# A graph-network block on one core: the batches of a software pipeline put in another order

## The chip, the cores and the metric

The kernel runs on one core of a Trainium2 chip. The metric is the device time of one execution in microseconds, the median of three runs. Every time below comes from those runs or from one profiled execution.

## What is computed

6250 nodes with 256 features each, and 106250 edges with 96 features, sorted by the node they point to (`dst`). For every node the edges that point to it are reduced in three ways, and a two-layer network is applied:

```
h    = maximum(layernorm(x), 0)                      # 6250 x 256
out1 = segment_sum(edge, dst); out2 = segment_max(edge, dst); out3 = out1 / count
cat  = concatenate([h, out1, out2, out3, u[0]], axis=1)
y    = relu(cat @ W1 + b1) @ W2 + b2                 # hidden size 1024
out  = x + (y + h)
```

## The kernel before

**Tiles.** 6250 nodes make 49 tiles: tile i holds one node for each of the 128 partitions, and within a partition the nodes are sorted by their number of edges, and each rank makes a tile. The tables `LOW` and `CAP` (49 entries each) say, for every tile, how many edge slots are always full and how many there can be. A tile with LOW = k1 and CAP = k1 + k2 has k1 + k2 slots of 96 numbers per partition; the k2 last ones are masked. Tiles 0 to 3 have 15 slots, 4 and 5 have 16, 26 and 27 have 21, 42 and 43 have 28, and the five heavy ones, 44 to 48, have 29, 31, 32, 35 and 40.

**Groups and batches.** `BATCHES` (line 44) is a list of 15 batches. A batch is one or two groups, and a group is a pair of tiles with equal LOW and CAP, or one heavy tile. A batch is so two, three or four tiles wide. Each group has its buffer: `ell[g % 2]` for its edges and `es[g % 2]` for its masked ones (both show as `work` in the trace).

**Stages.** The program is a software pipeline over the batches, written out by hand for each engine. In stage s, TensorE runs the two matrix layers of batch s in eight chunks of 128 hidden units (`layer1` of chunk C, L527, L531 and L536; then `layer2` of chunk C - 2, L547 and L551), and at the end of chunks 2, 3, 5 and 6 it transposes the first to fourth tile of batch s + 1 (`transposes`, L512 and L515). Between them the other engines run, in the same stage and cut into the same eight steps m = 0 to 7:

- VectorE: `lo` of the chunk before in every step (L821); then for batch s + 1 the tree of the first group (`tree_mid` in step 0, `tree_tail` in step 1, L736), `output` of batch s - 1 (L852) and `tree_head` of the second group (L725) in step 2, `tree_mid` and `tree_tail` of the second group in steps 3 and 4, `in_lo` of each tile in steps 3, 4, 6 and 7 (L825), `moments` of batch s + 2 in step 5, `residual` in step 6 (L838, L843), `scales` of batch s + 2 and `tree_head` of its first group in step 7.
- ScalarE: `relu` of the chunk in every step (L407 and L409); `norm` (L419), `means` (L426, L427) and `in_hi` (L434) of batch s + 1; and `mask` (L398), one instruction for each masked slot of a tile: that of the first group of batch s + 2 in steps 4 to 6, that of its second group half in step 7 and half in step 0 of the next stage.
- GpSimd: the gathers. `gather_x` (L301) of batch s + 2, one for each tile; `gather_group` (L308) of group g + 2 as soon as the tree of group g is done, four transfers for a pair and two for a single tile; `scatter` (L322) of batch s - 1, one for each tile.

Every engine works through its own list in order. What ties them: `layer1(C)` waits for `relu(C - 2)`, `layer2(C)` for `lo(C)`, `relu(C)` for `lo(C - 1)`, `transposes` of a tile for its `norm`, its `means` and the `in_lo` of the tile before, `means` for the tree of its group, and `mask` for the gather of its group. So TensorE can be some two chunks ahead of VectorE, and no more.

Of the kernel before, what the change touches and what calls it, by code (L numbers as in the profile page):

```python
# [16 lines left out]
def gnn_block(nc, x, dst, edge, u, W1, b1, W2, b2, out):  # L17
# [23 lines left out]
           22, 22, 23, 23, 24, 24, 24, 24, 25, 25, 27, 27, 28, 28, 29, 31, 32, 35, 40]  # L41
    assert len(LOW) == len(CAP) == PER

    BATCHES = [[(4, 5)], [(6, 7)], [(8, 9), (44,)], [(10, 11), (45,)], [(12, 13), (46,)], [(14, 15), (47,)], [(16, 17), (48,)],
               [(18, 19), (42, 43)], [(20, 21), (40, 41)], [(22, 23), (38, 39)], [(24, 25), (36, 37)], [(26, 27), (34, 35)],
               [(28, 29), (32, 33)], [(0, 1), (2, 3)], [(30, 31)]]
    NB = len(BATCHES)
    NCH = NB * HC
    groups, tiles = [], []
    g_of, t_of = [], []  # L50
    for b, gs in enumerate(BATCHES):
        g_of.append(list(range(len(groups), len(groups) + len(gs))))
# [9 lines left out]
    NG = len(groups)  # L62
    assert all(len(gs) <= 2 for gs in BATCHES)
    ELL, ES = 56, 26
# [862 lines left out]
```

How the kernel before makes its waits and increments, by code:

```python
        @block.sync  # L233
        def _(sp):
            sp.dma_start(sd[0:SR, 0:SC], dst_sd).then_inc(sd_in, 16)
            sp.wait_ge(seam_free, 2)
            sp.wait_ge(sd_in, 16)
            sp.dma_start(dstp[0:NS, :], dst.rearrange("(r c) -> r c", c=STEP)).then_inc(dstp_in, 16)
            sp.dma_start(dstp[NS:NS + WIN // STEP, :], tail[:, :]).then_inc(dstp_in, 16)
            sp.dma_start(sd[0:SR - 1, SC:SC + 1], dst_sd[1:SR, 0:1], allow_slow_non_contiguous=True).then_inc(seam_in, 16)
            sp.wait_ge(win_in, 16)
            for c in range(0, KC, 2):
                sp.dma_start(raw1[:, c * H:(c + 2) * H].rearrange("p (c h) -> p c h", h=H),
                             W1[c * P:(c + 2) * P, :].rearrange("(c p) h -> p c h", p=P)).then_inc(w1_in, 16)
# [3 lines left out]
            sp.dma_start(w1u, W1[K:K + G, :]).then_inc(c_in, 16)  # L248
            sp.dma_start(u0[:, :], u[0:1, :].rearrange("a g -> g a"), allow_slow_non_contiguous=True).then_inc(c_in, 16)
            sp.dma_start(b1c[:, :], b1.rearrange("(c p) -> p c", p=P), allow_slow_non_contiguous=True).then_inc(c_in, 16)
            sp.dma_start(b2b[:, :], b2.rearrange("(a d) -> a d", a=1).broadcast_to([P, D])).then_inc(c_in, 16)
            sp.wait_ge(flag_ready, 1)
            general = sp.value_load(flag[0:1, 0:1], min_val=0, max_val=1)
            with sp.If(general > 0):
# [11 lines left out]
        @block.gpsimd  # L267
# [21 lines left out]
            pool.memset(bad[:, :], 0.0).then_inc(consts, 1)  # L289
            pool.wait_ge(row_ready, 1)
            pool.wait_ge(dstp_in, 32)
```

## Time and profile before

| | us |
|---|---|
| median of 3 runs (lowest, highest) | 577.2 (576.81, 577.95) |
| the profiled execution, its own time | 576.6 |
| its span | 574.4 |
| TensorE busy in matmuls | 481.2 (84%) |
| VectorE busy | 470.0 (82%) |
| ScalarE busy | 351.0 (61%) |
| GpSimd busy | 242.0 (42%) |
| mean granted TensorE clock | 0.978 |

The shares are means over stages with different limits. The table of 40 slices shows TensorE at 9 tenths or more from slice 19 on, and between 4 and 9 tenths from slice 4 to 18. The start of layer 1 of each batch in the trace of TensorE gives the borders of the stages, and the stretch between two borders can be asked for the busy time of each engine.

### The profile page before, as it was taken

To read this page: it belongs to the slowest core of one execution; us is meant where nothing else is said; L and a number is where in the kernel's file an instruction comes from. 1 tells how busy PE (TensorE), PEld (TensorE's weight loads), DVE (VectorE), ACT (ScalarE), POOL (GpSimd) and SP (SyncE) were. 2 spreads that over 40 slices of the span, in tenths; PEclk is the share of its full clock that TensorE was granted. 3 is DMA by queue.
4 is the path that set the end of the run, shared out by engine and by line. 5 is a ranking of instruction groups with operands and counts; after the bars stand their busy time and mean duration, and the time that the engine had idled before them with its cause. 6 is when DMAs were issued, how large, how long until landed. Compare 5 with 4: busy or idle time off the path is not lost.

```text
span 574.4 us, 8775 instructions
## 1 busy us (share of the span) xinstructions
PE 481.2 (84%) x3016; PEld 443.3 (77%) x3016; DVE 470.0 (82%) x888; ACT 351.0 (61%) x951; POOL 242.0 (42%) x251
## 2 busy tenths in 40 slices
PE   0020569889999999877999999999999999999991
PEld 0020559889999899867988888888888888888991
DVE  4896768898998999989999998999989889793220
ACT  0934638676768586684856757667577685743330
POOL 2055430716182746645277274571752714202021
PEclk9999979898999999998999999999999999999997
DMA  2935430525253454733446245441550524001010
GB/s 79 287 97 172 139 132 2 171 100 181 100 165 142 152 182 141 246 105 126 157 147 212 70 137 193 151 167 66 184 199 15 158 90 156 34 0 38 1 38 18
DMA packets 18836, 71.12 MB, mean 124 GB/s; under 512 B 4571, under 2 KB 5755, under 8 KB 18776
## 3 DMA queue, kind: packets, MB, share of 16 engines
q0 software_dynamic: 15408, 65.72, 34.1%
q1 hardware_dynamic: 3378, 4.79, 2.8%
q8 instruction: 24, 0.39, 0.3%
q14 instruction: 26, 0.21, 0.1%
HBM read 64.09 MB, written 6.85 MB: 124 GB/s over the span
## 4 chain that ended last, share of the span: by engine, by line
PE 60%; DVE 15%; DMA 8%; ACT 7%; issue 5%; POOL 3%; SPq 0%; DVEq 0%; POOLq 0%; ACTq 0%
PE l1ps L527 24%; PE l1ps L531 12%; PE yps L547 11%; DVE work L736 9%; DMA work<-in_edge_attr,idx 6%; PE yps L551 6%; PE tps L512 3%; PE l1ps L536 3%; ACT work L398 3%; POOL work L308 2%; ACT cat L373 2%; DVE cat L736 1%; POOL out_y L322 1%; DMA work<-in_dst 1%; DVE inl L825 1%
## 5 line engine op out<-in xcount | busy, mean ns | idle before, releaser
L308 POOL DMA_INDIRECT work<-in_edge_attr,idx x98 | 118.4, 1208 | 202.5 <-DVE cat L736 153.3
L527 PE MATMUL l1ps<-inh,w1h 128*128 128x512 f32 (+2 forms) x480 | 173.8, 368 | 2.1 <-ACT hh L409 1.4
L527 PE MATMUL l1ps<-inh,w1l 128*128 128x512 f32 (+2 forms) x480 | 169.3, 359 | 0.0
L736 DVE TENSOR_TENSOR work<-work 128x768 f32<-128x768 f32 (+14 forms) x174 | 151.4, 902 | 1.1
L407 ACT ACTIVATE hf<-l1ps,b1e 128x512 f32<-128x512 f32 (+2 forms) x120 | 72.6, 605 | 108.2 <-PE l1ps L536 108.0
L398 ACT ACTIVATE work<-work,mk 128x96 f32<-128x96 f32 x435 | 122.5, 367 | 26.3 <-DMA work<-in_edge_attr,idx 26.0
L531 PE MATMUL l1ps<-inl,w1h 128*128 128x512 f32 (+2 forms) x480 | 112.9, 358 | 0.0
L821 DVE TENSOR_TENSOR hl<-hf,hh 128x512 fp32r<-128x512 f32 (+2 forms) x120 | 71.3, 594 | 42.8 <-ACT hh L409 37.1
L527 PEld LDWEIGHTS l1ps<-inh,w1h 128*128 128x128 f32 x480 | 92.7, 193 | 10.5 <-issue 2.0
L322 POOL DMA_INDIRECT out_y<-xr,oidx x49 | 68.3, 1393 | 77.1 <-DVE xr L852 63.0
L527 PEld LDWEIGHTS l1ps<-inh,w1l 128*128 128x128 f32 x480 | 93.0, 194 | 7.8
L547 PE MATMUL yps<-w2h,hh 128*128 128x256 f32 x392 | 98.5, 282 | 0.0
L547 PE MATMUL yps<-w2l,hh 128*128 128x256 f32 x392 | 98.1, 281 | 0.0
L531 PEld LDWEIGHTS l1ps<-inl,w1h 128*128 128x128 f32 x480 | 85.6, 193 | 10.3
L547 PEld LDWEIGHTS yps<-w2h,hh 128*128 128x128 f32 x392 | 74.3, 190 | 2.6
L547 PEld LDWEIGHTS yps<-w2l,hh 128*128 128x128 f32 x392 | 74.4, 190 | 2.4
L409 ACT ACTIVATE hh<-l1ps,b1e 128x512 fp32r<-128x512 f32 (+2 forms) x120 | 72.0, 600 | 0.0
L725 DVE TENSOR_TENSOR work<-work 128x1344 f32<-128x1344 f32 (+15 forms) x52 | 71.1, 1367 | 0.9
L551 PE MATMUL yps<-w2h,hl 128*128 128x256 f32 x392 | 66.2, 282 | 2.5 <-DVE hl L821 2.5
L301 POOL DMA_INDIRECT xr<-in_x,nid x49 | 51.3, 1047 | 36.1 <-DVE nid L643 21.5
L512 PE MATMUL tps<-ident,cat 128*128 128x128 f32 x196 | 31.3, 284 | 41.5 <-ACT cat L427 38.4
L512 PEld LDWEIGHTS tps<-ident,cat 128*128 128x128 f32 x196 | 22.7, 145 | 44.9 <-DVEq L786 34.5
(126 smaller groups left out, 478.5 us busy)
## 6 DMA issues: line engine op xcount, KB each, us to landing
work<-in_L_gnn_W SPq DMA_DIRECT2D x3, 1024.0 KB, 7.4
work<-in_edge_attr,idx POOLq DMA_INDIRECT x98, 5.3
xr<-in_x,nid POOLq DMA_INDIRECT x49, 4.0
out_y<-xr,oidx POOLq DMA_INDIRECT x49, 3.1
work<-in_dst SPq DMA_DIRECT2D x1, 415.0 KB
dstp<-in_dst SPq DMA_DIRECT2D x1, 415.0 KB
work<-in_L_gnn_W SPq DMA_DIRECT2D x3, 128.0 KB, 7.5
xr<-in_L_gnn_W SPq DMA_DIRECT2D x1, 256.0 KB, 11.1
```

The costliest lines, as they stand in the source:

```text
L308: pool.indirect_dma_start(out=ell[g % 2][:, at:at + kk * F], out_offset=None, in_=edge, in_offset=bass.IndirectOffsetOnAxis(ap=idx[:, a + ...
L322: pool.indirect_dma_start(out=out, out_offset=bass.IndirectOffsetOnAxis(ap=oidx[:, i:i + 1], axis=0), in_=xr[:, b % XS, k, :], in_offset=None,
L398: last = act.activation(es[g % 2][:, at * F:(at + 1) * F], ell[g % 2][:, src:src + F], ACT.Copy, scale=mk[:, a + j, e:e + 1])
L407: act.activation(hf[C % 2][:, 0:cols], l1ps[C % 2][:, 0:cols], ACT.Relu, bias=b1e[:, m:m + 1])
L409: act.activation(hh[C % 3][:, 0:cols], l1ps[C % 2][:, 0:cols], ACT.Relu, bias=b1e[:, m:m + 1]).then_inc(hi_done, 1)
L512: pe.transpose(tps[:, ks(c)], cat[:, k, ks(c)], ident[:, :])
L527: pe.matmul(ps, wt[:, c, ks(m)], inh[b % 2][:, c, 0:cols], start=(c == 0 and wt is w1h), stop=False)
L531: pe.matmul(ps, w1h[:, c, ks(m)], inl[b % 2][:, c, 0:cols], start=False, stop=False)
L547: pe.matmul(ybank(b, j)[:, j % 2 * D:(j % 2 + 1) * D], hh[C % 3][:, ks(j)], wt[:, m, :], start=(m == 0 and j % 2 == 0 and wt is w2h), stop ...
L551: last = pe.matmul(ybank(b, j)[:, j % 2 * D:(j % 2 + 1) * D], hl[C % 3][:, ks(j)], w2h[:, m, :], start=False, stop=(m == HC - 1), skip_gro ...
L736: return V.tensor_tensor(out=slots(buf, n, per, 0, size // 2) if out_ is None else out_, in0=slots(buf, n, per, 0, size // 2), in1=slots(b ...
L821: V.tensor_tensor(out=hl[C % 3][:, 0:cols], in0=hf[C % 2][:, 0:cols], in1=hh[C % 3][:, 0:cols], op=ALU.subtract).then_inc(lo_done, 1)
```

## The change

Only the list of batches is another. The widths before are 2, 2, 3, 3, 3, 3, 3, 4, 4, 4, 4, 4, 4, 4, 2; now they are 2, 2, 2, 4, 4, 3, 3, 4, 3, 4, 3, 4, 4, 4, 3: the same count of each width. The pairs that stand together and the partner of each heavy tile change too; groups, tables and all functions stay as they are.

```diff
-    BATCHES = [[(4, 5)], [(6, 7)], [(8, 9), (44,)], [(10, 11), (45,)], [(12, 13), (46,)], [(14, 15), (47,)], [(16, 17), (48,)],
-               [(18, 19), (42, 43)], [(20, 21), (40, 41)], [(22, 23), (38, 39)], [(24, 25), (36, 37)], [(26, 27), (34, 35)],
-               [(28, 29), (32, 33)], [(0, 1), (2, 3)], [(30, 31)]]
+    BATCHES = [[(4, 5)], [(6, 7)], [(8, 9)], [(10, 11), (12, 13)], [(14, 15), (16, 17)], [(18, 19), (45,)], [(20, 21), (46,)],
+               [(28, 29), (42, 43)], [(22, 23), (47,)], [(30, 31), (40, 41)], [(24, 25), (48,)], [(32, 33), (38, 39)],
+               [(0, 1), (2, 3)], [(34, 35), (36, 37)], [(26, 27), (44,)]]
```

Two places show what it moves, both on VectorE. The first is steps 2 to 4 of the last stage in which TensorE runs a batch of two. Before, that is stage 1, and the batch that is made ready has three tiles, the third of them tile 44 (`hl` is `lo`, `work` the tree, `inl` is `in_lo`):

```order
L821 TENSOR_TENSOR hl<-hf,hh 128x256
L852 TENSOR_TENSOR xr<-yps,xr 128x512
L725 TENSOR_TENSOR work<-work 128x1056
L725 TENSOR_TENSOR work<-work 128x672
L821 TENSOR_TENSOR hl<-hf,hh 128x256
L825 TENSOR_TENSOR inl<-tps,inh 128x4x128
L736 TENSOR_TENSOR work<-work 128x1344
L736 TENSOR_TENSOR work<-work 128x480
```

Now it is stage 2, and the batch that is made ready has four tiles, with (12, 13) as its second group:

```order
L821 TENSOR_TENSOR hl<-hf,hh 128x256
L852 TENSOR_TENSOR xr<-yps,xr 128x512
L725 TENSOR_TENSOR work<-work 128x1536
L725 TENSOR_TENSOR work<-work 128x2x192
L821 TENSOR_TENSOR hl<-hf,hh 128x256
L825 TENSOR_TENSOR inl<-tps,inh 128x4x128
L736 TENSOR_TENSOR work<-work 128x2x864
L736 TENSOR_TENSOR work<-work 128x2x384
```

The single tile's tree gave way to a pair's, which goes on for one more tile in every step behind it, while `lo` stays 256 columns wide.

The second is steps 2 to 4 of stage 8. Before, TensorE runs a batch of four there, and (38, 39) is the second group of the next batch:

```order
L821 TENSOR_TENSOR hl<-hf,hh 128x512
L852 TENSOR_TENSOR xr<-yps,xr 128x512 x2
L725 TENSOR_TENSOR work<-work 128x1728
L725 TENSOR_TENSOR work<-work 128x2x672
L821 TENSOR_TENSOR hl<-hf,hh 128x512
L825 TENSOR_TENSOR inl<-tps,inh 128x4x128
L736 TENSOR_TENSOR work<-work 128x2x1152
L736 TENSOR_TENSOR work<-work 128x2x384
```

Now TensorE runs a batch of three, and the second group is (40, 41):

```order
L821 TENSOR_TENSOR hl<-hf,hh 128x384
L852 TENSOR_TENSOR xr<-yps,xr 128x512 x2
L725 TENSOR_TENSOR work<-work 128x1920
L725 TENSOR_TENSOR work<-work 128x2x672
L821 TENSOR_TENSOR hl<-hf,hh 128x384
L825 TENSOR_TENSOR inl<-tps,inh 128x4x128
L736 TENSOR_TENSOR work<-work 128x2x1248
L736 TENSOR_TENSOR work<-work 128x2x480
```

`lo` became 384 columns wide and the tree of the second group a little larger; the stage that has to cover it is TensorE's for three tiles, not for four. Stages 6 and 10 are now of the same kind.

## Rows read from the trace of the kernel before

**Rows 1.** Windows: stages 0 to 8 and 14, borders at layer 1 of each batch.

```profile
core 0: us, PE busy (x) PEld busy (x) DVE busy (x) ACT busy (x) POOL busy (x), PEclk, DMA share, GB/s
65.20:92.80 27.60, 21.39 (x151) 20.73 (x152) 20.89 (x51) 17.86 (x58) 9.17 (x10) 0.88 0.37 124
92.80:117.60 24.80, 21.45 (x169) 21.10 (x169) 22.69 (x43) 17.86 (x56) 12.70 (x11) 0.93 0.42 133
117.60:149.10 31.50, 29.42 (x187) 29.25 (x186) 28.52 (x61) 21.32 (x61) 12.49 (x11) 0.95 0.43 147
149.10:178.20 29.10, 28.63 (x193) 28.46 (x192) 26.92 (x51) 21.32 (x61) 14.74 (x12) 1.00 0.44 145
178.20:208.50 30.30, 28.98 (x194) 28.46 (x193) 28.60 (x55) 21.72 (x62) 16.52 (x13) 1.00 0.44 146
208.50:239.80 31.30, 28.93 (x193) 28.42 (x193) 30.02 (x56) 22.38 (x65) 16.42 (x13) 1.00 0.44 146
239.80:278.10 38.30, 31.32 (x199) 30.61 (x198) 33.81 (x53) 24.33 (x71) 20.34 (x17) 0.96 0.50 173
278.10:316.10 38.00, 37.45 (x217) 32.36 (x216) 36.04 (x61) 25.86 (x69) 20.96 (x16) 1.00 0.44 150
316.10:353.90 37.80, 37.80 (x223) 33.05 (x221) 34.61 (x56) 25.53 (x68) 20.26 (x16) 1.00 0.44 151
...
541.90:563.00 21.10, 20.85 (x178) 20.65 (x176) 5.59 (x12) 6.73 (x17) 3.89 (x4) 1.00 0.07 26
```

**Rows 2.** TensorE's timeline in stage 0: first matmuls of two chunks, two tiles.

```profile
88.26 0.28 PE L527 MATMUL l1ps<-inh,w1h 128*128 128x256 f32 x1
...
90.49 0.28 PE L527 MATMUL l1ps<-inh,w1h 128*128 128x256 f32 x1
```

**Rows 3.** Chain that ended last: start, us; chunks of three tiles, then four.

```profile
171.68 1.39 PE l1ps L527 x8
...
175.01 1.41 PE l1ps L527 x8
...
344.61 1.87 PE l1ps L527 x8
...
347.64 0.95 PE yps L547 x8
348.59 0.47 PE yps L551 x4
...
349.61 1.87 PE l1ps L527 x8
...
354.06 1.87 PE l1ps L527 x8
```

**Rows 4.** Groups of instructions by form, VectorE: two sizes of the tree.

```profile
L725 DVE TENSOR_TENSOR work<-work 128x1344 f32<-128x1344 f32 x18 | 28.0, 1555 | 0.2
L736 DVE TENSOR_TENSOR work<-work 128x384 f32<-128x384 f32 x41 | 22.5, 550 | 0.1
```

**Rows 5.** VectorE's timeline in stage 6: first `lo`, then two tree pieces of (42, 43).

```profile
242.86 0.56 DVE L821 TENSOR_TENSOR hl<-hf,hh 128x384 fp32r<-128x384 f32 x1
...
253.25 3.74 DVE L725 TENSOR_TENSOR work<-work 128x2112 f32<-128x2112 f32 x2
...
258.10 4.08 DVE L736 TENSOR_TENSOR work<-work 128x2688 f32<-128x2688 f32 x2
```

**Rows 6.** TensorE's timeline: waits before transposes, one in stage 1, two in stage 6.

```profile
101.76 0.63 PE L512 MATMUL tps<-ident,cat 128*128 128x128 f32 x4 [2.18 <-ACT cat L427]
...
252.94 0.63 PE L512 MATMUL tps<-ident,cat 128*128 128x128 f32 x4 [1.93 <-ACT cat L427]
...
268.72 0.63 PE L512 MATMUL tps<-ident,cat 128*128 128x128 f32 x4 [2.97 <-ACT cat L427]
```

**Rows 7.** GpSimd's timeline: first gather of group (42, 43).

```profile
231.90 1.28 POOL L308 DMA_INDIRECT work<-in_edge_attr,idx  x1 [1.31 <-DVE cat L736]
```

**Rows 8.** ScalarE's timeline: first half of that group's mask.

```profile
243.36 3.04 ACT L398 ACTIVATE work<-work,mk 128x96 f32<-128x96 f32 x11 [3.37 <-DMA work<-in_edge_attr,idx]
```

**Rows 9.** GpSimd's timeline: the last scatter of the run.

```profile
565.55 0.97 POOL L322 DMA_INDIRECT out_y<-xr,oidx  x1 [0.30 <-issue]
```

## The prediction

> **What bounds the kernel now.** I read first the busy time by stage [rows 1], since the shares of the whole run mix stages with different limits. Behind the window and its length stand the busy times of PE, PEld, DVE, ACT and POOL, then TensorE's granted clock. What has to be seen is how much of a stage is more than TensorE needs at its full clock. That need comes from the starts of successive chunks: a chunk of a batch of two takes 90.49 - 88.26 = 2.23 us [rows 2], of three 175.01 - 171.68 = 3.33, of four 354.06 - 349.61 = 4.45, and 349.61 - 344.61 = 5.00 where a tile is transposed behind it, so 0.55 for a tile [rows 3]. Layer 2 is 0.95 + 0.47 = 1.42 us of a chunk of four, 0.355 for a tile, and the first two chunks of a stage carry layer 2 of the batch before. So a stage needs 8 chunks + 0.55 x (tiles of the next batch) + 0.71 x (width before - own width). For stage 8 this gives 35.6 + 2.2 = 37.8, which is its length to the tenth [rows 1]. The other stages, length less need:
>
> - stage 0: 27.6 - 17.6 = 10.0 (nothing precedes it: 1.4 less); stage 1: 24.8 - 19.6 = 5.2; stage 2: 31.5 - 27.6 = 3.9; stage 3: 29.1 - 28.4 = 0.7; stage 4: 30.3 - 28.4 = 1.9; stage 5: 31.3 - 28.4 = 2.9; stage 6: 38.3 - 28.9 = 9.4; stage 7: 38.0 - 37.1 = 0.9; stages 8 to 13: nothing; stage 14: 21.1 - 20.7 = 0.4.
>
> Together 35.3 us are lost, all but 1.3 in stages 0 to 6. The rest is TensorE's work, and that is the same in both orders: the same count of each width. So the change can give at most 35 us, and it is worth what it does to these losses.
>
> Next, who takes them. In stage 6 VectorE is busy 33.8 us against TensorE's need of 28.9: it runs three tiles and makes four ready. TensorE waits there before transposes, 1.93 and 2.97 us among others [rows 6], for `means`, which wait for the tree; two steps of the tree take 3.74 and 4.08 us [rows 5]. In stage 8 VectorE is busy 34.6, but TensorE needs 37.8 and covers it. Stages 1 to 5 are nearly even (VectorE 22.7 to 30.0), with losses to match. The rule to take along: a stage loses where the batch that runs is narrower than the batch that is made ready. Before this happens twice (2 to 3 tiles in stage 1, 3 to 4 in stage 6). The new order does it four times: 2 to 4 in stage 2, 3 to 4 in stages 6, 8 and 10.
>
> Two more things add to stage 6. VectorE enters it late: the stage begins at 239.8, its first `lo` at 242.86 [rows 5], 3 us behind. And the gather of (42, 43), issued from 231.90 [rows 7], is there only at 243.36, where the mask has made ScalarE wait 3.37 us [rows 8]; `relu` is queued behind that mask, and `lo` and TensorE's next chunks behind `relu`. Last, the clock: the stages with long waits show a granted clock of 0.88 to 0.96, the others 1.00 [rows 1]; in stage 6, 4% of 38.3 is 1.5 us, part of its 9.4.
>
> **The change stage by stage** (new losses).
>
> - Up to the end of stage 0: the first two batches and their gathers are the same, **10.0** stays. `moments` in it has one tile less, hidden behind the same waits.
> - Stage 1 (2 tiles, makes 2 ready): the work for tile 44 is gone. The 2.18 us wait of the first transposes [rows 6] is for (8, 9), and that stays. Bounds: 2.2, only this wait, and 5.2, no gain. I take **4.0**, nearer the upper end, as the halved clock comes with the wait.
> - Stage 2 (2 tiles, makes 4 ready) has no counterpart; the nearest is the old stage 1, VectorE busy 22.7 in 24.8. A size of the tree costs 0.15 us + 1.05 ns for an element: (1555 - 550) / 960 from two forms [rows 4]. By this the tree of (12, 13) is 8.3 us against 7.2 for tile 44: + 1.1; one more `in_lo` + 0.6, `residual` + 0.5, `moments` + 0.45, the rest + 0.35. So 25.7 busy and the same 2.1 idle: 27.8 against a need of 17.8 + 2.2 = 20.1, 7.7 lost. The edges of (14, 15), asked for in step 4 some 9 us after their gather is issued, can come late by 1 to 2 us, since such a gather takes 11.5 [rows 7, 8]; in return VectorE may end late into the wide stage 3. I take **8.0**; bounds 5.0 (three more us spill into stage 3) and 11.0 (nothing spills, late edges in full and more clock).
> - Stages 3 to 5 (4 to 4, 4 to 3, 3 to 3): TensorE covers VectorE as in stage 8, save the last, like the old stage 3. **1.4** in place of 0.7 + 1.9 + 2.9; bounds 0.3 and 4.0.
> - Stage 6 (3 to 4) is the old stage 6 with (28, 29) for (18, 19): by the size rule 0.6 us more tree. But VectorE enters it some 2 us late, not 3, as stage 5 follows on a wide stage, and the mask waits less by some 2 us, half of it felt. **8.5**; bounds 6.0 and 10.0.
> - Stage 8 (3 to 4) need: 26.7 + 2.2 + 0.7 = 29.6. Here VectorE enters in step, at most 0.7 us late, since stage 7 is wide. I walk it from the start of the stage. Steps 0 to 4 hold five `lo` (2.5), the middle and tail of (30, 31) (6.7), `output` (1.2), all of the tree of (40, 41) (12.1), two `in_lo` (1.2): 23.7, done at 24.4, with `means` some 25. TensorE comes to the transposes of that group's first tile after six chunks, two transposes and the extra layer 2: 20.0 + 1.1 + 0.7 = 21.8. It waits 3 us. The last tile costs a few tenths, the halved clock behind the wait up to 1.5. **4.5**; bounds 1.5 and 9.4 (as the old stage 6).
> - Stage 10 (3 to 4): the tree of (38, 39) is 0.8 us less, but the mask of (0, 1), 26 slots in place of 14, stands in steps 4 to 6 on ScalarE, ahead of `in_hi` of the third tile. **5.0**; same bounds.
> - Stages 7, 9 and 11 to 14: at most the 0.9 of the old stage 7 each. **1.4** in all; bounds 0.5 and 3.0.
>
> New losses: 10.0 + 4.0 + 8.0 + 1.4 + 8.5 + 4.5 + 5.0 + 1.4 = 42.8, against 35.3: **+ 7.5**.
>
> - The end: three scatters in place of two behind the last `output`; one is 0.97 + 0.30 = 1.27 us [rows 9]. **+ 1.3**. The order of the other gathers moves no queue onto the path: GpSimd is busy at most 55% of a stage [rows 1], and its waits are for the tree.
>
> 576.6 + 7.5 + 1.3 = **585.4** for an execution like the profiled one. That one stands 0.6 us under the median of the runs, 577.2, less than they scatter; I keep 585.4.
>
> One rule weighed: the gather of (42, 43) moves 56 slots of 48 KB, 2.75 MB, and took 11.5 us from the first issue to the mask [rows 7, 8]. The Trainium skill (DMA: Bandwidth & Descriptors, Anatomy of one DMA — SWDGE (gpsimd) path) gives some 2.0 us fixed and the bytes at 436 GB/s, which makes an estimate of 8.3 us. By that no mask in stage 6 would wait and the sum would be some 1.5 us less, 583.9; the row decides.
>
> **Rivals.**
>
> 1. *The lag is absorbed, and the run gets faster.* TensorE may be two chunks ahead of VectorE, 6.7 us in a batch of three, and after each narrow stage a wide one follows in which VectorE catches up at some 3 us a stage (37.8 against 34.6). If waits begin only when those two chunks are used up, and not at the transposes, stages 8 and 10 lose 1.5 each, stage 6 6.0, stage 2 5.0, stage 1 2.2, the others 0.8: 27.0. The time is 576.6 - 8.3 + 1.3 = 569.6. For it: stages 1 to 5, where VectorE was 90% or more busy, lost little. Against: all three waits of [rows 6] are at transposes, which depend on VectorE directly. It decides if the third tile's `means` are done less than 22 us into stage 8. Chance 0.14.
> 2. *Each step from three to four costs what the old one did.* If lag, late mask and clock come back each time, stages 6, 8 and 10 lose 9.4 each, stage 2 11.0: 10.0 + 5.2 + 11.0 + 1.4 + 28.2 + 1.4 = 57.2, so 576.6 + 21.9 + 1.3 = 599.8. For it: the only sample. Against: that sample began 3 us late and with a late gather, which a wide stage before it should spare. Chance 0.18.
> 3. *The losses only change places*: early stages (2 to 5 lost 9.4) give what 8 and 10 take, and the time is 577 to 578. Chance 0.05.
>
> **Numbers.** The forecast gets 0.63. The likeliest case gives 585.4. The range goes from 573, which leaves out most of the first rival, to 600, which takes in the second to its price: 573 to 600. A measurement of this kernel tells about 0.2% (1.2 us). Faster by more: the first rival and a little of the forecast's lower side, 0.16; within: 0.04; slower: 0.80.
>
> **What would show it.** In the profile after: stages 6, 8 and 10 are 37.4, 34.1 and 34.6 us long, each with a wait of TensorE of 2 us or more before the transposes of the third tile; stage 2 is some 28 us with VectorE busy nearly throughout; stages 3, 4, 7, 9 and 11 to 13 have no waits worth naming; layer 1 of batch 0 begins at 65.2 as before. If stages 8 and 10 come out under 31 us the walk is wrong, and the slack between the engines is larger than I took it; if they are 38 or more, lag does not die out in a wide stage.

## The result and the profile after

The changed kernel takes 586.2 us (median of 4 runs, 585.36 to 586.5) against 577.58 for the kernel before in the same comparison: a ratio of 1.0147, interval 1.0132 to 1.0163. It is slower by 8.6 us. The prediction said 585.4, and 8.8 us more for an execution like the profiled one.

The same windows as in [rows 1], of the changed kernel, all 15 stages (columns as there):

```profile
65.50:94.40 28.90, 23.53 (x151) 23.14 (x152) 20.43 (x49) 17.96 (x58) 11.06 (x12) 0.88 0.40 129
94.40:115.70 21.30, 19.12 (x164) 18.95 (x164) 17.32 (x40) 13.78 (x41) 8.51 (x9) 1.00 0.34 107
115.70:143.90 28.20, 23.26 (x174) 22.89 (x173) 25.48 (x46) 20.81 (x65) 17.01 (x15) 0.88 0.51 162
143.90:181.20 37.30, 36.56 (x211) 31.67 (x210) 33.20 (x60) 25.14 (x66) 12.63 (x12) 1.00 0.35 115
181.20:218.50 37.30, 37.30 (x218) 32.55 (x217) 31.33 (x54) 22.57 (x59) 14.84 (x14) 1.00 0.36 124
218.50:247.60 29.10, 29.10 (x199) 29.10 (x199) 26.96 (x54) 20.95 (x58) 16.58 (x15) 1.00 0.51 171
247.60:284.60 37.00, 30.98 (x197) 30.47 (x197) 34.17 (x50) 24.38 (x71) 17.49 (x14) 0.95 0.44 150
284.60:321.10 36.50, 36.50 (x211) 31.75 (x210) 33.66 (x63) 23.63 (x62) 17.69 (x14) 1.00 0.44 155
321.10:356.10 35.00, 31.70 (x205) 31.36 (x205) 32.38 (x51) 24.02 (x69) 18.30 (x14) 0.95 0.43 146
356.10:392.60 36.50, 36.50 (x211) 31.77 (x211) 34.52 (x60) 25.02 (x68) 19.95 (x15) 1.00 0.46 152
392.60:426.30 33.70, 30.15 (x204) 29.64 (x203) 30.88 (x48) 25.99 (x78) 18.90 (x16) 1.00 0.38 116
426.30:465.00 38.70, 37.52 (x217) 32.45 (x216) 34.86 (x64) 27.42 (x75) 17.04 (x15) 1.00 0.45 151
465.00:503.10 38.10, 37.87 (x221) 32.97 (x221) 35.71 (x54) 24.70 (x65) 13.95 (x10) 1.00 0.31 106
503.10:540.40 37.30, 37.30 (x218) 32.55 (x217) 26.77 (x39) 18.36 (x41) 5.82 (x4) 1.00 0.04 14
540.40:570.20 29.80, 29.80 (x202) 29.61 (x200) 6.45 (x11) 8.45 (x17) 3.90 (x4) 1.00 0.05 19
```

Where TensorE's busy time (first after the comma) is the stage's length, nothing or nearly nothing is lost: stages 4, 5, 7, 9, 13, 14. Apart from the start (stages 0 and 1), the stages in which a narrow batch runs while a wider one is made ready (2, 6, 8, 10) are those with a large gap. With the need of each stage from the prediction's rule:

| stage | widths | lost, forecast | lost, measured |
|---|---|---|---|
| 0 | 2 to 2 | 10.0 | 28.9 - 17.5 = 11.4 |
| 1 | 2 to 2 | 4.0 | 21.3 - 18.9 = 2.4 |
| 2 | 2 to 4 | 8.0 | 28.2 - 20.0 = 8.2 |
| 3 to 5 | 4, 4, 3 to 3 | 1.4 | 1.0 |
| 6 | 3 to 4 | 8.5 | 37.0 - 28.8 = 8.2 |
| 8 | 3 to 4 | 4.5 | 35.0 - 29.6 = 5.4 |
| 10 | 3 to 4 | 5.0 | 33.7 - 29.6 = 4.1 |
| 7, 9, 11 to 14 | | 1.4 | 2.3, of it 1.6 in stage 11 |
| all | | 42.8 | 43.0 |

These are all waits of TensorE in stages 6, 8 and 10, from its timeline (the bracket is the idle time before the row, and what ended it); they answer to [rows 6]:

```profile
259.40 0.63 PE L512 MATMUL tps<-ident,cat 128*128 128x128 f32 x4 [1.61 <-ACT cat L427]
264.87 0.63 PE L512 MATMUL tps<-ident,cat 128*128 128x128 f32 x4 [1.42 <-DVE inl L825]
275.28 0.63 PE L512 MATMUL tps<-ident,cat 128*128 128x128 f32 x4 [2.99 <-ACT cat L427]
...
336.69 0.63 PE L512 MATMUL tps<-ident,cat 128*128 128x128 f32 x4 [0.73 <-DVE inl L825]
346.68 0.63 PE L512 MATMUL tps<-ident,cat 128*128 128x128 f32 x4 [2.57 <-ACT cat L427]
...
408.13 0.63 PE L512 MATMUL tps<-ident,cat 128*128 128x128 f32 x4 [0.75 <-DVE inl L825]
417.51 0.63 PE L512 MATMUL tps<-ident,cat 128*128 128x128 f32 x4 [1.93 <-ACT cat L427]
422.44 0.63 PE L512 MATMUL tps<-ident,cat 128*128 128x128 f32 x4 [0.86 <-DVE inl L825]
```

All are before transposes, and the longest of each stage is that of the third tile (275.28, 346.68, 417.51), as the walk through stage 8 had it.

VectorE enters stage 8 only 322.18 - 321.1 = 1.1 us behind, with the `lo` of the last chunk of four tiles, and stage 10 0.8 us behind (393.41 - 392.6). It enters stage 6 3.2 us behind (250.76 - 247.6), like the old stage 6 [rows 5]:

```profile
250.76 0.56 DVE L821 TENSOR_TENSOR hl<-hf,hh 128x384 fp32r<-128x384 f32 x1
...
322.18 0.69 DVE L821 TENSOR_TENSOR hl<-hf,hh 128x512 fp32r<-128x512 f32 x1
```

At the end stand three scatters, the last issued at 574.30 against 565.55 before [rows 9]; from the end of TensorE's work to the end of the last scatter's issue it is 575.3 - 570.2 = 5.1 us against 566.5 - 562.8 = 3.7.

### The profile page after: what moved, and what is told of

The parts are those of the page before. It is cut to its first block, busy times and chain, and to the rows that moved or that the text cites. A ratio compares the mean times of both kernels' runs of the same rounds, so it can differ in the third digit from the quotient of the medians.

```text
span 583.2 us, 8775 instructions
## 1 busy us (share of the span) xinstructions
PE 484.2 (83%) x3016; PEld 446.8 (77%) x3016; DVE 471.3 (81%) x888; ACT 351.1 (60%) x951; POOL 238.2 (41%) x251
## 4 chain that ended last, share of the span: by engine, by line
PE 61%; DVE 17%; ACT 8%; DMA 5%; issue 4%; POOL 2%; SPq 0%; DVEq 0%; POOLq 0%; ACTq 0%
PE l1ps L527 24%; PE l1ps L531 12%; PE yps L547 12%; DVE work L736 9%; PE yps L551 6%; PE tps L512 4%; DMA work<-in_edge_attr,idx 3%; ACT work L398 3%; PE l1ps L536 3%; ACT cat L373 2%; DVE work L725 2%; POOL work L308 2%; DVE inl L825 1%; DVE cat L736 1%; DMA work<-in_dst 1%
## 5 line engine op out<-in xcount | busy, mean ns | idle before, releaser
L308 POOL DMA_INDIRECT work<-in_edge_attr,idx x98 | 115.8, 1181 | 210.3 <-DVE cat L736 178.7
L736 DVE TENSOR_TENSOR work<-work 128x576 f32<-128x576 f32 (+11 forms) x174 | 151.7, 903 | 1.1
L322 POOL DMA_INDIRECT out_y<-xr,oidx x49 | 66.0, 1347 | 79.6 <-DVE xr L852 65.6
L512 PE MATMUL tps<-ident,cat 128*128 128x128 f32 x196 | 32.5, 292 | 47.6 <-ACT cat L427 41.6
```

The source lines that it names most:

```text
L308: pool.indirect_dma_start(out=ell[g % 2][:, at:at + kk * F], out_offset=None, in_=edge, in_offset=bass.IndirectOffsetOnAxis(ap=idx[:, a + ...
L512: pe.transpose(tps[:, ks(c)], cat[:, k, ks(c)], ident[:, :])
L736: return V.tensor_tensor(out=slots(buf, n, per, 0, size // 2) if out_ is None else out_, in0=slots(buf, n, per, 0, size // 2), in1=slots(b ...
```

## The experiments

The first four ran together on one chip (12), with the kernel before beside them at 578.46 us. The changed kernel was not among them, so the ratio to the kernel before is what is compared: 1.0147 for the changed kernel. A difference of 1 to 2 us found in this way is small: the kernel before itself stood 0.9 us higher here than in the first comparison. So the traces are set beside it; that of the changed kernel has a span of 583.2 us and loses 43.0.

A single stage is less steady than the whole. These are two stages 1 that run the same program, of the run with fewer masks below and of the changed kernel on a later chip; in the changed kernel's first trace the stage takes 21.30 us at a granted clock of 1.00:

```profile
93.80:116.70 22.90, 20.72 (x164) 20.55 (x163) 17.32 (x40) 13.81 (x41) 9.56 (x10) 0.93 0.34 105
...
95.80:121.00 25.20, 21.91 (x165) 21.72 (x164) 17.66 (x41) 14.12 (x43) 9.80 (x10) 0.86 0.33 103
```

So the same stage loses 2.4, 4.0 or 6.2 us, TensorE's busy time rises with the loss, and its granted clock falls. Stage 6 loses 8.2 in the changed kernel's first trace and 6.9 in the run with fewer masks, which leaves it alone.

**VectorE's work taken out of the narrow stages** (part of the computation is left out)

```diff
+    LIGHT = (3, 7, 9, 11)
 ...
                 dve.wait_ge(masked, g + 1)
+                if g in [g_of[b][1] for b in LIGHT]:
+                    V.tensor_tensor(out=s[:, 0:1], in0=s[:, 0:1], in1=e[:, 0:1], op=ALU.add).then_inc(dve_step, 1)
+                    dve.wait_ge(dve_step, next(step))
+                    return
```

> The changed kernel without the first piece of the tree (L725) of the second group of batches 3, 7, 9 and 11, the four whose preparation stands in a stage narrower than they are; one column is added in its place, so that the output of these tiles is not the reference's. This takes 2.3 + 3.7 + 3.6 + 3.4 = 13.0 us from VectorE. Theory A (VectorE's work in the narrow stage is what TensorE waits for): stages 2, 6, 8 and 10 lose 8.1, 8.2, 5.3 and 4.2 us now and fall by 2 to 3.5 each, 10 to 12 us in all, so about 575. Theory B (late gathers and masks on ScalarE hold these stages): under 3 us less, 583 or more.

Measured: 574.67 us, ratio 0.9938 (0.9921 to 0.9955). Against 1.0147 that is 2.1% or 12.1 us less, for 12.6 us less of VectorE's busy time (458.7 against 471.3). Windows of stages 2, 6, 8 and 10:

```profile
115.60:142.40 26.80, 22.25 (x175) 21.73 (x174) 23.42 (x45) 21.32 (x68) 14.85 (x14) 0.94 0.52 166
246.10:279.10 33.00, 30.88 (x198) 30.53 (x198) 30.09 (x47) 24.25 (x71) 16.49 (x14) 0.95 0.46 161
315.60:346.40 30.80, 29.88 (x205) 29.71 (x204) 28.02 (x46) 24.15 (x69) 17.14 (x14) 1.00 0.45 160
383.10:415.00 31.90, 30.00 (x205) 29.66 (x204) 27.85 (x47) 25.95 (x78) 18.55 (x16) 1.00 0.40 123
```

They are 1.4, 4.0, 4.2 and 1.8 us shorter than in the changed kernel. VectorE's busy time in them is less by 2.1 to 4.4 us, GpSimd's by 0.4 to 2.2, and ScalarE's is the same within 0.5. The sum came out as expected; of the single stages two gave more than the 2 to 3.5 expected, and two less.

The edit also lets the gathers behind these trees start sooner, so the waits of ScalarE for edges have to be looked at. In stage 2 that wait fell by 1.1 us, from 2.59 to 1.49, and the stage gained 1.4: there the two causes can't be told apart. In stages 6, 8 and 10 the waits grew, from 2.08 to 2.48, from none to 0.44 and from 0.59 to 1.37, while the stages became shorter:

```profile
133.77 1.44 ACT L399 ACTIVATE work<-work,mk 128x96 f32<-128x96 f32 x5 [1.49 <-DMA work<-in_edge_attr,idx]
...
248.81 3.04 ACT L399 ACTIVATE work<-work,mk 128x96 f32<-128x96 f32 x11 [2.48 <-DMA work<-in_edge_attr,idx]
...
403.28 2.24 ACT L399 ACTIVATE work<-work,mk 128x96 f32<-128x96 f32 x8 [1.37 <-DMA work<-in_edge_attr,idx]
```

So Theory B falls for stages 6, 8 and 10.

**The same work taken out of wide stages** (the same edit for batches 4, 8, 10 and 13; part of the computation is left out)

> The same piece left out for the second group of batches 4, 8, 10 and 13, whose preparation stands in a stage that is at least as wide (stages 3, 7, 9 and 12), some 10.5 us of VectorE's work; the output of these tiles is not the reference's. Theory A: those stages are TensorE's and lose 0.9, 0, 0 and 0.4 us, so at most 1.3 us less, 585 to 586. Rival C (VectorE's total counts, wherever it stands): 8 to 10 us less, 577.

Measured: 585.11 us, ratio 1.0121 (1.0104 to 1.0138), 1.5 us less than the changed kernel by the ratios, with intervals that overlap. Stages 3, 7 and 9 keep their length to the tenth, stage 12 loses nothing in place of 0.4, and the span of the trace is 583.2 as in the changed kernel. VectorE's total is nearly the same before and after the change (470.0 and 471.3 us); 9.3 us taken from it are worth at most 1.5 in one place, 12.6 are worth 12 in the other. Rival C falls.

**Fewer masks on ScalarE** (part of the computation is left out)

```diff
+                first, end = n * k2 * piece // pieces, n * k2 * (piece + 1) // pieces
+                if g in [g_of[b][1] for b in (9, 11)]:
+                    end = first + 1
-                for at in range(n * k2 * piece // pieces, n * k2 * (piece + 1) // pieces):
+                for at in range(first, end):
```

> The changed kernel with 2 masks each in place of 20 and 18 for the second groups of batches 9 and 11, so 34 instructions and some 9.5 us less on ScalarE, at the borders of stages 7/8 and 9/10; the output of these tiles is not the reference's. Theory A: 0 to 1.5 us less, since relu follows a mask only in step 0. Theory B: stages 8 and 10 lose their 9.5 us of waits, 577 to 580.

Measured: 586.09 us, ratio 1.0137 (1.0118 to 1.0157): no difference that can be told, for 9.2 us less of ScalarE's busy time (341.9 against 351.1). Stage 8 loses 5.4 as before, and stage 10 4.7 where it lost 4.1. The masks in steps 4 to 6 were left as they are, so this says nothing of them.

**One step up in place of three**

```diff
-               [(28, 29), (42, 43)], [(22, 23), (47,)], [(30, 31), (40, 41)], [(24, 25), (48,)], [(32, 33), (38, 39)],
+               [(22, 23), (47,)], [(24, 25), (48,)], [(28, 29), (42, 43)], [(30, 31), (40, 41)], [(32, 33), (38, 39)],
```

> The changed order with batches 8 and 10 moved to stand behind batch 6, so that the widths are 2,2,2,4,4,3,3,3,3,4,4,4,4,4,3 and there is one step from three to four in place of three. Theory A: the losses of stages 8 and 10 (5.3 + 4.2) go, two stages from three to three cost 2 to 3 each, and the one step that is left costs 8.5 to 9.5, as VectorE enters it late: about 4 us less, 582. Rival 1 of the prediction (lag is absorbed anyway): no change, 586. If steps were all that counted and stages from three to three cost nothing: 577.

Measured: 584.93 us, ratio 1.0114 (1.0096 to 1.0132), 1.9 us less by the ratios; expected were 4. In the traces the losses are 42.4 in place of 43.0, so most of the 1.9 may be noise. Its stages 6 to 9, with widths 3 to 3, 3 to 3, 3 to 4, 4 to 4:

```profile
249.40:279.80 30.40, 28.94 (x193) 28.42 (x192) 28.47 (x52) 21.63 (x62) 15.51 (x13) 1.00 0.43 151
279.80:312.30 32.50, 29.03 (x193) 28.52 (x192) 30.80 (x57) 22.46 (x65) 16.39 (x14) 1.00 0.45 153
312.30:349.40 37.10, 31.13 (x198) 30.59 (x197) 34.48 (x52) 24.30 (x71) 18.82 (x16) 0.95 0.47 164
349.40:388.90 39.50, 37.58 (x216) 32.35 (x216) 37.40 (x64) 26.42 (x71) 21.75 (x17) 1.00 0.48 165
```

The one step costs 37.1 - 28.8 = 8.3, close to the 8.5 that the prediction had for a step that VectorE enters late. But the two stages from three to three cost 2.1 and 4.2, since they make the batches with tiles 47 and 48 ready, and the wide stage behind the step still loses 2.4, which I had left out: VectorE is busy 37.4 us in it and pays off what it owes. Narrow stages in a row build up a debt; alternating ones pay it each time. So the number of steps up is not what counts by itself: these four stages lose 17.0 us with one step, and stages 6 to 10 of the changed kernel 17.7 with three.

**The step up early, and the narrow batches behind the wide ones.** Two orders that follow from theory A. The first begins with two batches of two, so that its step up stands in stage 1; the second begins with one, so that it stands in stage 0. This is the second:

```diff
+    BATCHES = [[(4, 5)], [(8, 9), (10, 11)], [(22, 23), (42, 43)], [(24, 25), (40, 41)], [(26, 27), (38, 39)], [(28, 29), (36, 37)],
+               [(30, 31), (34, 35)], [(0, 1), (2, 3)], [(12, 13), (48,)], [(14, 15), (47,)], [(16, 17), (46,)], [(18, 19), (45,)], [(20, 21), (44,)],
+               [(32, 33)], [(6, 7)]]
```

> A new order with the same groups' sizes: widths 2,2,4,4,4,4,4,4,4,3,3,3,3,3,2, so one step up (2 to 4, in stage 1, with the light pairs (8, 9) and (10, 11)) and from there on no stage narrower than the batch it makes ready. Theory A: stage 0 loses 10 to 11, stage 1 8 to 9.5, the stages of four together 3, the four from three to three 1 to 2 each, the end as before: 28 in all against 35 before, so 5 to 9 us faster than the kernel before, ratio 0.984 to 0.991. Rival C (the total of VectorE's work counts, whatever the order): as before, 1.00.

Measured: 575.76 us (8 runs), ratio 0.9953 (0.9936 to 0.997): faster than the kernel before by 2.7 us, where 5 to 9 were expected. Its trace is of its slowest run (578.11). Stage 1 loses 8.2, as expected, but stage 0 12.5, stage 2 4.5, and stages 10 to 13 3.0, 1.4, 2.5 and 3.9.

> The same with the step up already in stage 0: widths 2,4,4,4,4,4,4,4,3,3,3,3,3,2,2. Theory A: stage 0 takes on the work for two more tiles (some 11 us of VectorE's) on top of its 10 us, of which part are waits in which the work does not fit: it loses 17 to 21; stage 1 nothing, the two stages of two at the end 0 to 2. In all 27 to 32: 0.984 to 0.995 of the kernel before.

Measured: 570.55 us, ratio 0.9868 (0.9854 to 0.9883): inside the expectation, and 7.7 us faster than the kernel before. The parts were partly luck. Stage 0 with four tiles to make ready loses 12.6, not 17 to 21; but stage 1, which was to lose nothing, loses 4.5, like the stage behind the step in the order before. The two together make 17.1: part of the debt is paid one stage on.

Both orders also change which groups stand together and put the heavy tiles into the narrow batches, and both end with two scatters in place of three, like the kernel before. What they share cancels between the two of them: the step in stage 0 in place of stage 1 is worth 5.2 us.

**Two repairs of the changed order that gave nothing**

```diff
+                    late = 1 if s == 2 else 0
-                    if 4 <= m < 7 and ahead:
-                        mask(ahead[0], m - 4, 3)
+                    if 4 + late <= m < 7 + late and ahead:
+                        mask(ahead[0], m - 4 - late, 3)
```

> The changed kernel with the three pieces of the mask of (14, 15) in stage 2 in steps 5, 6 and 7 in place of 4, 5 and 6, so that ScalarE does not wait for their edges (2.59 us) ahead of means. VectorE ends the tree of (12, 13) at 135.1, the transposes start at 137.0: stage 2 gets 1.1 us shorter, the rest the same: 0.5 to 1.5 us less than the changed kernel. If the late edges were the whole wait: 2.7 us less.

> The changed order with batches 12 and 13 in exchange, so that the 26 masks of (0, 1) stand in stage 11 (four tiles) and no more in stage 10 (three tiles). The prediction put 0.5 to 1.2 us of stage 10 down to them. Theory A: stage 10 loses 3.2 to 4.0 in place of 4.2, and the 1.5 of stage 11 goes: 1 to 2 us less in all. If masks do not count: no change.

Measured: 593.42 us for both, ratios 1.0258 (1.0242 to 1.0274) and 1.0265 (1.0249 to 1.028), 7 us above the changed kernel where 0.5 to 2 below were expected. They and the two orders before ran together on another chip (13). The exchanged order is slower already in stages 0 to 2, where its program is that of the changed kernel. So I ran four kernels side by side once more.

> The order with batches 12 and 13 in exchange once more. In its first run it took 593.4 us, and its trace shows what no trace before it shows: TensorE's signal that a chunk is ready reached ScalarE 2 to 5 us after the last matmul of the chunk at a dozen places, stage 0 among them, in which its program is that of the changed kernel. Theory D (those late signals come with the chip or the load, not with the order): 584 to 585.5 us now, no such late signal, stage 10 at 3.2 to 4.0 us of loss. Rival E (they belong to this kernel's program): 593 again.

> The changed kernel once more, beside the others. Theory D: like its first runs, 586, unless this chip shows the late signals, and then in all four kernels of this call. Rival E: 586 while the exchanged order stays at 593.

> The kernel before as a kernel of its own, for its trace on this chip: 577 to 579 us; its trace shows late signals only if Theory D's chip is the one that is drawn.

> The order with the step up in stage 0 once more. It took 570.6 us with a dozen late signals. Theory D: without them the stages of four tiles lose nothing, and the run is 3 to 7 us shorter, 563 to 567. Rival E: 570.5 again.

Measured, on chip 10: the exchanged order 592.56 us (1.0248), the changed kernel itself 592.74 (1.0235, 1.0214 to 1.0256), the kernel before 578.39 (0.9998), the step up in stage 0 570.40 (0.9859). So rival E falls: the changed kernel is at 593 here too. Theory D's first half fits: the late signals are in all four kernels that ran here, and in none of chip 12. Its numbers fell, since this chip showed them too. But each chip was used for one set of runs, so the chip and anything else that went with the set can't be told apart. `relu` in stage 0 on ScalarE's timeline, the changed kernel in its first trace:

```profile
83.47 0.47 ACT L407 ACTIVATE hf<-l1ps,b1e 128x256 f32<-128x256 f32 x1 [2.18 <-PE l1ps L536]
87.13 0.47 ACT L407 ACTIVATE hf<-l1ps,b1e 128x256 f32<-128x256 f32 x1 [0.68 <-PE l1ps L536]
89.36 0.48 ACT L407 ACTIVATE hf<-l1ps,b1e 128x256 f32<-128x256 f32 x1 [0.33 <-PE l1ps L536]
```

and on chip 10:

```profile
83.75 0.47 ACT L407 ACTIVATE hf<-l1ps,b1e 128x256 f32<-128x256 f32 x1 [2.18 <-PE l1ps L536]
90.33 0.47 ACT L407 ACTIVATE hf<-l1ps,b1e 128x256 f32<-128x256 f32 x1 [3.48 <-PE l1ps L536]
92.13 0.46 ACT L407 ACTIVATE hf<-l1ps,b1e 128x256 f32<-128x256 f32 x1
```

TensorE's timeline has the last matmul of that chunk at 86.81 in the first and at 86.68 on chip 10; there `relu` starts 3.4 us after it ends. Of what `relu` waits for, the `lo` of VectorE had ended at 85.0, so it isn't that:

```profile
86.68 0.28 PE L536 MATMUL l1ps<-inr,w1r 96*128 96x256 f32 x1
```

Differences of a few us can be read only between kernels that ran together. Beside the changed kernel on chip 10 the exchanged order gains 0.2 us, within the noise. Its stage 10 loses 4.9 in place of 5.8, and its stage 11 2.0 in place of 1.6. Beside the later mask on chip 13, which leaves these stages as they were, stage 10 loses 5.6 in place of 5.7. So what the 26 masks of (0, 1) cost in stage 10 lies between nothing and some 1 us, and isn't settled; the prediction's sum has 1.3 for them (5.0 - 4.5 + 0.8).

The later mask shortens the wait that it was made for: in stage 2 the third tile waits 1.70 us, against 2.48 in the exchanged order beside it. In stage 3 the first tile now waits 2.55 us, against 0.73 in the changed kernel's first trace, and the stage loses 4.9 in place of 0.9. VectorE's `tree_head` had waited 2.12 us for the mask there. How much of that is the edit's isn't shown, since a late signal stands in front of the same mask (`relu` at 149.83, after 1.83 us).

## Why the prediction was right

- **The rule.** A stage loses where the batch that runs is narrower than the one made ready: all four places came out, within 1 us each, and no other stage but 0, 1 and 11 lost more than 1. The pair of runs without `tree_head` shows that it is VectorE's work in stages 6, 8 and 10; in stage 2 the late edges may have a part. That each stage hit within 1 us is in part luck, since a stage of the same program moved by 1.3 to 3.8 us between traces.
- **The walk through stage 8.** It had the tree of (40, 41) done at 24.4 us into the stage and the wait for the third tile at 3 us; in the trace the last piece of that tree ends at 345.8 - 321.1 = 24.7, and the wait is 2.57, as TensorE comes 1.2 us later than in the walk. VectorE was 1.1 us behind at the start where 0.7 was taken. The lag does die out in a wide stage, which fits stage 8's 5.4 against the old 9.4. Rival 1 falls (the third tile's `means` came after 22 us), rival 2 falls, and so does rival 3, which had the time at 577 to 578. One sign just missed: stage 10's wait is 1.93, not 2 or more.
- **Stage 6.** 37.0 us, forecast 37.4, but not by the forecast's way. VectorE was to enter it 2 us late and entered it 3.2 us late, and the mask's wait was to be some 2 us shorter and was 1.3 us shorter. Both would have made it more than 8.5; it lost 8.2. The gather of (42, 43) took its 11.4 us again (issued at 238.45, its mask at 249.81 after a wait of 2.08 us). So the row was the right price. By the formula of the Trainium skill (DMA: Bandwidth & Descriptors, Anatomy of one DMA — SWDGE (gpsimd) path) the estimate had been 8.3 us, and this trace doesn't agree with it. The four issues alone, which follow one another on GpSimd, take 5.1 us here (238.45 to 243.51).
- **Stage 2.** 28.2 us, forecast 28.1. The late edges of (14, 15) made ScalarE wait 2.59 us there, more than the 1 to 2 I had.
- **Stages 0 and 1** missed by 1.4 and 1.6, in opposite directions. In stage 1 the halved clock that I had charged did not come in this trace: its granted clock is 1.00. In two runs of chip 12 (fewer masks, and one step up in place of three), with the same program there, it is 0.93 and the stage loses 4.0, as forecast. In stage 0 the halved clock came while TensorE worked and not while it waited. Two windows, 75 to 80 and 80 to 85, of the kernel before:

```profile
75.00:80.00 5.00, 1.69 (x7) 1.42 (x8) 3.49 (x8) 1.76 (x6) 1.22 (x2) 0.51 0.00 0
80.00:85.00 5.00, 5.00 (x37) 5.00 (x36) 1.92 (x4) 2.38 (x6) 3.51 (x4) 0.81 0.91 311
```

and of the changed one:

```profile
75.00:80.00 5.00, 1.15 (x5) 0.97 (x6) 3.71 (x9) 1.51 (x6) 0.97 (x2) 0.84 0.00 0
80.00:85.00 5.00, 5.00 (x26) 4.99 (x25) 1.54 (x3) 1.76 (x4) 3.78 (x5) 0.50 0.85 258
```

- **Stage 11** lost 1.6 where nearly nothing was forecast, as the lag of stage 10 spills over; the "rest" of 1.4 was too small by 0.9. **The end**: + 1.3 forecast, + 1.4 measured. **The start**: layer 1 of batch 0 begins at 65.5, not at 65.2.

So the sum hit within 1 us partly because errors of up to 1.6 cancelled. And it holds for the first comparison: on chip 10 the change costs 2.35% (592.74 us), which the range still takes in.

## What to carry to other kernels

In a pipeline that works on batch s and makes batch s + 1 ready, look at the width of the batch that is made ready against the width of the one that runs. Where the first is the larger, the engine that prepares has more work than the stage covers (here such stages lose 4 to 8 us each), and its slack in a wide stage before can't be saved up. Merging the steps up into one is not enough: one step behind two narrow stages cost nearly as much as three steps. What helped was to put the step into the start, where the bound engine waits anyway; that order is 1.3% faster than the kernel before, and on chip 10, beside it, 3.8% faster than the changed one (570.40 against 592.74 us). And balance by the stage in which the work is done, not by the total.

## What was not expected of the hardware

In the traces of chips 13 and 10, ScalarE starts `relu` late at 5 to 10 places of a run: it waits for nothing else that the trace shows, and starts 0.1 to 3.4 us after the last matmul of its chunk ends. At the other places where it waits for that matmul, and at all of them in the first comparison's and chip 12's traces, it is under 0.1 us, mostly 0.04. Some updates of that signal are missing in the late traces (110 to 116 of 121 are recorded), but the late `relu` at 90.33 is a record of its own. Counted so, the late places are fewer and shorter than the dozen of 2 to 5 us that I had written down before the last runs.

The kernel before takes 577.6 to 578.5 us in all four comparisons. Its trace on chip 10 has such late signals too: stages 0, 1, 3 and 7 lose 3.7 us more there, and stages 2 and 6 4.3 us less. The changed kernel pays 6.5 us, and its stages 0 to 2 are 7.8 longer: they lose 12.5, 6.2 and 11.1. Not all of this is the late signal itself: in stage 1 TensorE is busy 2.8 us longer, at a granted clock of 0.86 in place of 1.00, and in stage 2 the mask waits 3.73 us for its edges in place of 2.59. What delays the signals, whether it is the chip, how much of the 6.5 us they explain, and why the total of one order doesn't move, stays open; it wasn't tried.
